# A selective-scan kernel on one core: another split of the products by B between GpSimd and ScalarE, and another order around slot 12

## The reference

```python
def _mamba_block(x, p):
    xn = _rmsnorm(x, p['norm_w'])
    xz = xn @ p['Win']
    xp, z = jnp.split(xz, 2, axis=-1)
    xc = jax.nn.silu(_causal_depthwise_conv(xp, p['conv_w'], p['conv_b']))
    dbc = xc @ p['Wx']
    dt, Bm, Cm = jnp.split(dbc, [DT_RANK, DT_RANK + D_STATE], axis=-1)
    delta = jax.nn.softplus(dt @ p['Wdt'] + p['bdt'])
    y = _selective_scan(xc, delta, -jnp.exp(p['A_log']), Bm, Cm, p['Dp'])
    return x + (y * jax.nn.silu(z)) @ p['Wblk']

# one step of the scan
dA = jnp.exp(d_t[:, :, None] * A)
h = dA * h + (d_t * u_t)[:, :, None] * b_t[:, None, :]
y = jnp.einsum('bdn,bn->bd', h, c_t)
```

## Time and profile before

| what | us |
|---|---|
| median of 3 runs | 2141.58 |
| lowest and highest | 2139.24 and 2146.53 |
| the profiled execution, its own time | 2140.07 |
| its span, first to last instruction | 2138.3 |
| PE busy (share of the span) | 1856.2 (87%) |
| DVE busy | 1861.6 (87%) |
| ACT busy | 1682.8 (79%) |
| POOL busy | 1362.5 (64%) |
| scans on DVE, 512 of them | 1160.8 |

### The profile page before, as it was taken

One profiled execution on the slowest core, in us unless ns is written; L12 is line 12 of the kernel. 1 busy time (PEld: TensorE's weight loads), 2 busy tenths in 40 slices (PEclk: granted clock), 3 DMA queues, 4 the chain that ended last, 5 costly groups with the idle time before them and its releaser, 6 DMA issues.

```text
span 2138.3 us, 34563 instructions
## 1 busy us (share of the span) xinstructions
PE 1856.2 (87%) x10816; PEld 1170.8 (55%) x10816; DVE 1861.6 (87%) x1762; ACT 1682.8 (79%) x3053; POOL 1362.5 (64%) x1428
## 2 busy tenths in 40 slices
PE   4788888888888888888888888888887799999998
PEld 1444444444444444444444444444444499989998
DVE  3799999999999999999999999999999987767775
ACT  4899999899999999999999999999898443333333
POOL 2688888888888888887788888888887600000000
PEclk9899999999999999999999999999999999999999
DMA  7323232323232323232333333232323200000000
GB/s 243 84 66 80 63 79 62 79 62 79 62 79 63 79 66 81 66 80 71 76 80 76 80 77 82 68 79 62 79 62 73 84 2 11 11 11 10 10 6 11
DMA packets 72777, 138.41 MB, mean 65 GB/s; under 512 B 13072, under 2 KB 31120, under 8 KB 68112
## 3 DMA queue, kind: packets, MB, share of 16 engines
q1 hardware_dynamic: 66320, 119.28, 23.0%
q10 hardware_dynamic: 6400, 18.42, 3.7%
HBM read 63.85 MB, written 7.74 MB: 33 GB/s over the span
## 4 chain that ended last, share of the span: by engine, by line
PE 59%; ACT 16%; DVE 15%; issue 6%; ACTq 1%; POOL 1%; SPq 1%; DMA 1%; DVEq 0%; POOLq 0%
PE dbu_ps L1087 13%; PE y_ps L1312 11%; PE pre_ps L1100 10%; PE dbu_ps L1286 8%; PE y_ps L1069 7%; DVE scan L844 7%; ACT decay L577 6%; DVE dbu_ps L844 5%; ACT scan L655 3%; PE pre_ps L1110 3%; PE pre_ps L1117 2%; PE pre_ps L1165 2%; DVE scan L854 2%; ACT sp_l L624 2%; PE y_ps L1187 1%
## 5 line engine op out<-in xcount | busy, mean ns | idle before, releaser
L492 POOL TENSOR_TENSOR scan<-scan,c_rep 128x1024 f32<-128x1024 f32 x319 | 754.6, 2371 | 138.3 <-DVE scan L844 120.0
L1087 PE MATMUL dbu_ps<-ident,scan 128*128 128x128 f32 x4096 | 559.2, 282 | 239.3 <-DVE scan L844 170.1
L1087 PEld LDWEIGHTS dbu_ps<-ident,scan 128*128 128x128 f32 x4096 | 473.9, 144 | 508.9 <-DVE scan L844 192.5
L844 DVE TENSOR_TENSOR_SCAN scan<-decay,dbu_ps 128x1024 f32<-128x1024 f32 x320 | 722.7, 2275 | 22.9 <-PE dbu_ps L1087 22.8
L577 ACT ACTIVATE decay<-d_rep,a_cur 128x510 f32<-128x510 f32 x1024 | 667.9, 709 | 60.7 <-ACT dbc L601 16.9
L844 DVE TENSOR_TENSOR_SCAN dbu_ps<-decay,dbu_ps 128x1024 f32<-128x1024 f32 x192 | 438.1, 2282 | 93.4 <-PE dbu_ps L1087 91.2
L655 ACT ACTIVATE scan<-du_t,b_t 128x256 f32<-128x256 f32 x1024 | 445.3, 494 | 1.3 <-PE dbu_ps L1087 0.2
L486 POOL TENSOR_SCALAR scan<-du_t,b_t 128x256 f32<-128x256 f32 x896 | 416.0, 484 | 0.0
L780 ACT ACTIVATE decay<-dbu_ps 128x512 f32<-128x512 f32 x256 | 148.0, 598 | 206.8 <-PE dbu_ps L1286 184.4
L1069 PE MATMUL y_ps<-scan,sel 128*32 128x512 f32 x2048 | 301.0, 663 | 0.0
L1100 PE MATMUL pre_ps<-xn,w_pre 128*128 128x512 f32 x512 | 245.5, 603 | 5.3 <-DVE w_pre L832 5.3
(11 more groups left out here) (112 smaller groups left out, 1748.2 us busy)
## 6 DMA issues: line engine op xcount, KB each, us to landing
d_rep<-delta SPq DMA_DIRECT2D x496, 128.0 KB, 2.9
c_rep<-c_rows SPq DMA_DIRECT2D x32, 1024.0 KB
w_pre<-prepared_weights ACTq DMA_DIRECT2D x15, 866.0 KB, 13.4
prepared_weights<-scan SPq DMA_DIRECT2D x3, 1122.0 KB, 11.7
scan<-in_conv_w SPq DMA_DIRECT2D x4, 512.0 KB, 5.0
w_out<-prepared_weights SPq DMA_DIRECT2D x16, 128.0 KB, 12.8
sp_e<-in_x_rows SPq DMA_DIRECT2D x8, 256.0 KB, 3.0
d_rep<-in_w ACTq DMA_DIRECT2D x2, 1024.0 KB, 6.6
```

The source lines that it names most:

```text
L492: nc.gpsimd.tensor_tensor(ring[slot % RING], ring[slot % RING], c_rep[par][:, slot // PRS, :].unsqueeze(1).broadcast_to([128, 2, TG]), ALU ...
L844: nc.vector.tensor_tensor_scan(states.rearrange("p u t -> p (u t)"), decay[slot % DEC].rearrange("p u a t -> p (u a t)"), dbu_ps[slot % 2] ...
L1087: last = nc.tensor.transpose(dbu_ps[slot % 2][:, u, 128 * j:128 * j + 128], dbu_t[m % 2][:, j, b, :, :].rearrange("p q c -> p (q c)"), ide ...
```

## The change

GpSimd makes ten of a group's sixteen products: both j for every state as before, and j = 2 for the states q of 0 and 2. ScalarE makes the other six, two in each of three slots. `POOL_SHARE` is now 5, 3, 2 and none, `POOL_FIRST` none, 5, 3, 2. The waits of GpSimd's `outer` are now issued only where there is a product to make, so those for group 0 stand at slot 13, behind the product by C of slot 11. On PE the fourth `quad` and `turn_du` move from slot 11 to slot 12, behind that slot's `to_channels`.

```diff
-POOL_OUTER = Q * POOL_J
-ACT_OUTER = Q * (JT - POOL_J)
-SHARE = (0, 2, 5, 8)
-FIRST = (0, 3, 6, 8)
-POOL_SHARE = (0, 2, 3, 4, 4)
-POOL_FIRST = (0, 0, 2, 3, 4)
+POOL_BLOCKS = tuple((q, j) for q in range(Q) for j in range(JT) if j < POOL_J or j == POOL_J and q % 2 == 0)
+ACT_BLOCKS = tuple((q, j) for q in range(Q) for j in range(JT) if (q, j) not in POOL_BLOCKS)
+POOL_OUTER = len(POOL_BLOCKS)
+ACT_OUTER = len(ACT_BLOCKS)
+SHARE = (0, 2, 4, 6)
+FIRST = (0, 2, 4, 6)
+POOL_SHARE = (0, 5, 8, 10, 10)
+POOL_FIRST = (0, 0, 5, 8, 10)
+QUAD_SLOTS = (5, 7, 9, 12, 13, 15)
...
-                if first == 0:
+                if first == 0 and last:
                     wait(pool, dbu_ready, SLOTS * s + PRS * (m - 1))
...
-                for q, j in itertools.product(range(first, last), range(POOL_J)):
+                for q, j in POOL_BLOCKS[first:last]:
...
-                for n in range(first, last):
-                    q, j = n // (JT - POOL_J), POOL_J + n % (JT - POOL_J)
+                for q, j in ACT_BLOCKS[first:last]:
...
-                    if has(s, 0) and slot >= 5 and slot % 2:
-                        quad(s, (slot - 5) // PRS, (slot - 5) % PRS // 2)
+                    if has(s, 0) and slot in QUAD_SLOTS:
+                        pair = QUAD_SLOTS.index(slot)
+                        quad(s, pair // KT, pair % KT)
...
-                    if slot == 11 and has(s, 1):
+                    if slot == 12 and has(s, 1):
                         turn_du(s + 1)
```

## The result

| | before | changed |
|---|---|---|
| median of 4 runs each, us | 2144.06 (2139.24 to 2146.77) | 2107.59 (2105.98 to 2110.84) |
| ratio, 95% interval | | 0.9852 (0.9834 to 0.987) |
| profiled execution: its time, span | 2140.07, 2138.3 | 2108.24, 2106.4 |
| mean step, slot 0 to slot 0, 28 steps | 51.24 | 50.42 |

The time came out within 2 us of the forecast. What follows shows that the sum was righter than its parts. Both come from the one profiled execution of each kernel, while the ratios come from all of its executions.

A forecast was written before the change was run, and what follows sets the result against it. VectorE, busy nearly all the time within steps, was taken as the bound, with waits at slots 8 and 12. 0.80 + 0.64 - 0.10 - 0.25 = 1.09 us a step, 32.7 us over 30 steps, gave 2109 us (2100 to 2124).

The forecast's parts named there:

- Experts' part and start are not touched: Outside the steps: the change was to alter nothing in the experts' part or the start.
- ScalarE's two products, 0.80: Between the copy of dbc and slot 8's decay: two products fewer on ScalarE, gain 0.80 us a step.
- Slots 12 and 0, 0.64: Slot 12's wait (1.39 and 1.80 us) goes, 0.43 and 0.85 return at slot 0: gain 0.64 us a step.
- the clock, -0.10: PE behind its pause: the lower clock may last longer; bounds nothing and 1.4 us a step, taken as -0.10.
- GpSimd's chain: From du's start to the next step's first transposes: GpSimd works without a pause, 17.47 us with the hand-over.
- the half microsecond that PE was to have to spare: Ahead of slot 0: PE ready at 932.3, GpSimd's products at 932.84, so PE has 0.5 us to spare.
- the slower rival: PE's lower clock lasts till slot 14: a step loses 1.5 us, 2187 us in all; chance 0.08.
- Collisions, -0.25: At softplus: GpSimd's later products hold up VectorE; bounds nothing and 1.0 us a step, taken as -0.25.
- the two fewer in other slots lie beside other work and I cost them at nothing: ScalarE's other dropped products: no gain counted, since ahead of slot 4 ScalarE waits for PE's projections.
- behind the transposes of slot 11 come the four matmuls of a sum: PE ahead of slot 12: the sum and du's transposes precede slot 12's transposes, so its scans come 1.39 to 1.80 us late.

The follow-up runs named there:

- e5: The changed kernel with GpSimd making eight products instead of ten for group 3 only; ratio to the kernel before 0.9879.
- e3: The kernel before with PE's new order and GpSimd's wait moved, split of eight and eight kept; ratio to the kernel before 1.0003.
- e10: The kernel before with 18 matmuls of zeros in PE's pause behind slot 10, old order and split; ratio to the kernel before 0.9831.
- e1: The kernel before with the split of ten and six alone, PE's order and GpSimd's wait as before; ratio to the kernel before 0.9988.
- e2: The kernel before with PE's new order alone, split and place of GpSimd's wait as before; ratio to the kernel before 1.0031.
- e7: The changed kernel with PE's fourth sum moved from slot 12 into PE's pause at slot 10; ratio to the kernel before 0.9839.
- e12: e9 with 12 matmuls of zeros behind the sum in PE's pause; median 2095.85 us, ratio to the kernel before 0.98.
- e9: The changed kernel with ten and six for group 2 only, eight and eight elsewhere, and the fourth sum at slot 10; ratio to the kernel before 0.9822.
- e8: The changed kernel with 28 matmuls of zeros in PE's pause behind slot 10; ratio to the kernel before 0.9858.

## Why the prediction was right, and where it was not

The forecast was a gain of 1.09 us a step. The profile has 0.82 (51.24 - 50.42), which makes 25 us in 30 steps, and the two spans differ by 31.9. The rest was there before the second step: its slot 0 comes at 106.75 us instead of 114.71. In the first step before, a decay of ScalarE waits 4.61 us for a DMA of `d_rep`, and slot 3 then waits 7.17 us; after, these are 2.69 and 0.31. Over all profiles the wait at slot 3 of the first step lies anywhere from 0.3 to 7.2 us, so I can't say that the change made it. "Experts' part and start are not touched" was therefore not true of the two executions compared, and the closeness of the total was luck by these 8 us: the steps gave three quarters of what was forecast for them.

- **ScalarE's two products, 0.80.** Measured 0.81 (1.28 to 0.47): the decay of slot 8 is earlier by just the two products.
- **Slots 12 and 0, 0.64, and the clock, -0.10.** Slot 12 has no wait, slot 0 has 0.79 and slot 13 0.34. 1.57 - 0.79 - 0.34 = 0.44, where 0.54 were forecast. GpSimd's chain was right to 0.14 us in the step shown and to 0.02 in the mean; the term that was mis-sized is the clock's, with the half microsecond that PE was to have to spare. The sum stood at the half clock and du's transposes partly: together 953.67 - 950.78 = 2.89 us, where 2.3 were counted, and slot 13 waits behind them (0.34, where the term was 0.10). Slot 0's transposes start 17.78 us behind du in the mean, 0.31 later than the forecast's 17.47: in 14 of the 28 steps more than 0.25 us, and up to 1.61, behind GpSimd's last product, so there PE decides and not GpSimd. The mean granted clock of the steps fell from 0.95 to 0.94. It is a part of the slower rival, which I gave 0.08 as a whole.
- **Collisions, -0.25.** Measured -0.16. The first softplus instruction takes about 1.47 us in 14 of the 28 steps (1.44 to 1.50), and in 10 of the others the second takes 1.30. e5 shows that GpSimd's products of group 3 do it: without the added two, all are back at 1.22. It shows too that this term can't be had back by itself (0.03 us a step). The Trainium skill's rule of the port pair that only one of the two engines holds (page "SBUF — State Buffer", section "SBUF: two separate sides") asks for such a term; the trace agrees.
- **Small waits at slots 2 to 4**, not forecast, take 0.19 and with these the sum is 0.81 + 0.44 - 0.16 - 0.19 = 0.90, near the 0.82.

Two steps of the working failed, and the total hides it.

The first is the sentence that "the two fewer in other slots lie beside other work and I cost them at nothing". It counted ScalarE's slack as it was before. The new order spends that slack: du's copies come 1.56 us later behind du in the mean (8.69 instead of 7.13), and without the four products fewer ahead of silu the gain of 0.64 is zero (e3). The rule for such a step would be: what one part of a change hides behind must be looked up again after the other parts are in.

The second is the cause of the wait at slot 12. I read it as a wrong order, "behind the transposes of slot 11 come the four matmuls of a sum", with the clock as a side term. The order makes it only together with the half clock: at the full clock the old order has no wait (e10), and at the half clock the split alone loses at slot 12 what it wins at slot 8 (e1). The terms were added as if each could be had alone; the split (e1) and the order with the moved wait (e3) gain nothing each, and the two together, which are the change, gain 1.5%.

What stays open: why e1, e2 and e3, with different waits, have steps of 51.21, 51.21 and 51.22 us, within 0.03 of before. Each is explained by its own rows; a cause common to them was not looked for beyond these.

## What to carry to other kernels

When a wait stands a few us behind a pause of TensorE, read the granted clock there before blaming the order: filling the pause with zeros (e10) is a small edit and was worth as much as the whole change (0.9831 and 0.9852, with intervals that overlap). Moving work that is due anyway into the pause (e7) shortened the steps too, though PE still fell to the half clock behind it. The two remedies did not add up: with the wait already gone, the fill gave 0.10 us a step (e12 against e9). When a change has several parts, cost each engine's chain with all of the parts in place, since slack that hides one part may be spent by another. And when the parts have been measured singly at nothing, that says little about them together.

## What the runs showed of the hardware

- Eighteen matmuls of zeros in a pause of each step raised the mean granted clock of the steps from 0.95 to 1.00, and the kernel before became 1.7% faster though PE was busy for longer (1117 us instead of 1030 in the same stretch of 1200).
- 28 matmuls of 128x64 by 128x128 zeros in float32 took 6.33 us at the full clock (e8, granted clock 1.00), 0.23 each.
- VectorE's instruction with two inputs in SBUF is held up by 0.25 us (1.47 instead of 1.22) or 0.08 (1.30) where it meets GpSimd's products of 128x256, less than one whole product (0.46); without the two added products it is not (e5).
